# Attention matmuls on 128x32 column tiles in a four-layer convolution kernel

## The chip, the cores and the metric

The kernel runs on one core of a Trainium2 chip. The metric is the device time of one execution in microseconds (us), given as the median of several runs. A profile is one more execution, recorded by the hardware profiler.

## The reference

The input x is four images of 32 channels by 32x32 pixels, in float32. Four residual layers follow each other, each as x = x + layer(norm(x)), where norm normalises every channel of every image by its mean and variance:

```
x = x + L0(norm(x))   # second-order Volterra convolution 3x3: 9 taps and 45 products of tap pairs
x = x + L1(norm(x))   # 3x3 convolution (written with FFTs)
x = x + L2(norm(x))   # gated cell fed by attention
x = x + L3(norm(x))   # mixing of channels between two Hartley transforms
```

The change lies in the attention of L2. The cell's hidden state is zero, so one attention remains of four:

```
q = conv(xin, Wq, 'SAME')    # (4, 4 heads, 8, 1024 queries)
k = conv(xin, Wk, 'VALID')   # (4, 4 heads, 8, 900 keys)
v = conv(xin, Wv, 'VALID')
w = softmax(q^T k)           # over the 900 keys
a = v w^T
```

The gates i, g and o are then a projection of a, a bias and a sigmoid or a tanh, and the layer ends in a 32x32 projection.

## The kernel before

Five engines run their own instruction streams and meet at semaphores: TensorE (PE) does matrix products into PSUM, ScalarE (ACT) and VectorE (DVE) read PSUM, GpSimd (POOL) and SyncE (SP) issue copies, and POOL does some elementwise work.

The attention is computed for eight halves `s` (four images, two halves of 512 queries each). Queries and keys are split into three bfloat16 parts each, so that a product has 72 contraction rows and keeps float32 accuracy. For each half there are four kinds of PE work:

- Blocks of maxima (`max_block`, matmul at L1134): 128 queries against 450 keys. They find each query's maximum before the exponential. For each of the 16 pairs of head and query tile of a half there are two blocks. Either both are read by DVE, each by a reduction (L874), or the first is a product with the difference of two key halves, which goes through a ReLU on ACT (L669) and is then added to the second and reduced in one DVE instruction (L869). In halves 0 and 1 all 16 go by way of ACT, later 6 of 16.
- The turn (`turn_maxima`, L1141): the 48 columns of split maxima are transposed, so that they can be added to the contraction as three more rows. DVE copies the result and POOL issues a copy that places it.
- Score tiles (`score_tile`): 29 a half. 28 of them are 128 keys against 512 queries of one head (L1158); the 29th holds the 4 last keys of all four heads as four matmuls on 32 columns each (L1163). ACT takes the exponential of each (L661).
- Values (`values`): eight groups a half. The first seven have four matmuls, one head each, on 32 columns each (L1176); the eighth is one matmul on 128 columns (L1181). They are in float32, and the profile shows two instructions for each float32 matmul.

A PE instruction on the whole array is written 128*128 (or 72*128, rows in use by columns); one that uses 32 of the columns is written 128*32, and four of these address the four column strips of the array. Each matmul has a weight load (LDWEIGHTS, shown as the engine PEld) ahead of it.

The order of all this work is written out by `attention_plan()` (L132). A step of a half is four scores, of which the third is followed by the values of the step before, and between them 4.34 blocks of maxima (`BLOCKS_PER_STEP`) of the half after or the one after that. Every engine walks the same plan. Scores rotate over three PSUM banks (`SCORE_RING`), blocks of maxima and the turn over three others (`MAX_RING`), values over two. A score waits until the exponential of the third score before it has ended; a block waits until the block three before it has been read. Ahead of the first score 46 blocks and the first turn run, and 41 of these blocks are followed by a filler matmul on zeros (`keep_clock`). The gates (L1240, on 32 columns) and the output projection (L1248, on 128 columns) of the first 512 queries lie inside the last half.

Of the kernel before, what the change touches and what calls it, by code (L numbers as in the profile page):

```python
# [38 lines left out]
BF16 = mybir.dt.bfloat16  # L39
# [5 lines left out]
P = 128  # L45
B, C, H, W = 4, 32, 32, 32
# [43 lines left out]
HEADS, HC = 4, 8  # L90
# [3 lines left out]
KHALF = KEYS // 2  # L94
# [6 lines left out]
PARTS = 3  # L101
PAIR_ROWS = PARTS * PARTS * HC
S_ROWS = PAIR_ROWS + PARTS
HALF_TILES = HALF // P
ROWS_OF_MAX = HEADS * HALF_TILES
EXP_UNITS = HEADS * DT + 1
PRING = 8
# [24 lines left out]
def attention_plan():  # L132

    stream, i = [], 0
    for s in range(2 * B):
        for a in range(ROWS_OF_MAX):


            pair = s < 2 or a % 8 in (0, 3, 6)  # L150
            for kind in (("diff", "first") if pair else ("first", "second")):
                stream.append(("max", i, s, a, kind))
                i += 1
        stream.append(("split", s))
        if s == 2 * B - 1:
            stream += [("pause",)] * MOVED
        stream.append(("turn", i, s))
        i += 1

    for at in [at for at, item in enumerate(stream) if item[0] == "turn"]:  # L160
        if stream[at][2] == 0:
            continue
        n = min(MOVED, len(stream) - 1 - at)
        moved = stream[at + 1:at + 1 + n] + [stream[at]]
        numbers = sorted(item[1] for item in moved)
        stream[at:at + 1 + n] = [(item[0], k, *item[2:]) for item, k in zip(moved, numbers)]
    plan = []

    def take(n):

        while n > 0 and stream:
            item = stream.pop(0)
            if item[0] != "pause":
                plan.append(item)
            if item[0] != "split":
                n -= 1

    take(2 * ROWS_OF_MAX + 1 + FIRST_AHEAD)
    due, prev, later, step = 0.0, None, [], 0
    for s in range(2 * B):  # L180
        for t in range(DT + 1):
            units = HEADS if t < DT else 1
            due += BLOCKS_PER_STEP * (1.0 if t < DT else 0.6)
            taken = 0
            for h in range(units):
                plan.append(("score", s * EXP_UNITS + t * HEADS + h))
                k = int(due * (h + 1) / units + 1e-6)
                take(k - taken)
                taken = max(taken, k)
                if prev and h == min(2, units - 1):  # L190
                    plan.append(("values", *prev))
            due -= taken
            if prev and prev[1] == DT:
                later += [(step, ("read", prev[0])), (step + 1, ("write", prev[0]))]
                if prev[0] == 2 * B - 2:

                    later += [(step + 1, ("gates", 0)), (step + 2, ("cell", 0)), (step + 3, ("hidden", 0)),
                              (step + 4, ("out", 0))]
            plan += [item for at, item in later if at <= step]
            later = [(at, item) for at, item in later if at > step]  # L200
            prev = (s, t)
            step += 1
    plan += [("values", *prev)] + [item for _, item in later]
    plan += [("read", prev[0]), ("write", prev[0])]
    plan += [("gates", 1), ("cell", 1), ("gates", 2), ("hidden", 1), ("cell", 2), ("out", 1), ("hidden", 2),
             ("out", 2)]
    assert not stream
    return plan
# [28 lines left out]
def build(nc, x, consts, wmodes, max_rows, out):  # L237
    ctx = ExitStack()
    with ctx:
# [17 lines left out]
        vrest = sb("vrest", [P, B, P])  # L257
# [7 lines left out]
        mparts = sb("mparts", [P, PARTS, ROWS_OF_MAX], BF16)  # L265
        mt_sb = sb("mt_sb", [PARTS * ROWS_OF_MAX, P], BF16)
        ident_b = sb("ident_b", [P, P], BF16)
# [15 lines left out]
        qst = arena_a[:, 0:q_words].bitcast(BF16).rearrange("p (e g n) -> p e g n", e=2, g=G)  # L283
        kst = arena_a[:, q_words:q_words + k_words].bitcast(BF16).rearrange("p (g n) -> p g n", g=G)
# [9 lines left out]
        at = B * H * WP  # L294
# [7 lines left out]
        at = 8192 + PARTS * HW // 2  # L302
# [5 lines left out]
        probs = arena_b[:, 0:PRING * HALF].rearrange("p (s n) -> p s n", n=HALF)  # L308
# [7 lines left out]
        ps = ctx.enter_context(nc.psum_tensor("ps", [P, 8, 512], F32))  # L316
# [59 lines left out]
        max_scored = sem("max_scored")  # L376
# [55 lines left out]
            return maps[:, m, :].rearrange("p (y x) -> p y x", x=WP)[:, y0:y1_, x0:x1_]  # L432

        plan = attention_plan()
        prologue = 2 * ROWS_OF_MAX + WIDE_AHEAD

        def block_bank(i):

            ring = SCORE_RING + MAX_RING if i < prologue else MAX_RING
            return ring[i % len(ring)]  # L440
# [542 lines left out]
        def _(pe):  # L983
            mm = nc.tensor.matmul
# [63 lines left out]
            for i in range(3):  # L1048
                for r in range(3):
                    at = r * WP + i * PLANE  # L1050
                    last = mm(ps[32 * r:32 * r + 32, 2 + i, 0:PLANE], c_("bsel"), xp[:, at:at + PLANE],
                              start=True, stop=True)
# [3 lines left out]
            for e in range(2):  # L1056
                pe.wait_ge(planes_ready, e + 2)
                for px in range(3):
                    last = mm(ps[:, e, :].rearrange("p (y x) -> p y x", x=W), l1s[:, px, :],  # L1059
                              window(planes[0:96, :], 0, px, 16 * e, 16, W), start=(px == 0), stop=(px == 2))  # L1060
# [7 lines left out]
            for n in range(2 * B):  # L1068
                e, b = divmod(n, B)
# [48 lines left out]
            for h in range(HEADS):  # L1118
                last = mm(ps[32 * h:32 * h + KREST, 1, 3 * P:4 * P], vs[:, DT * P:KEYS], c_("ident"),
                          start=True, stop=True)  # L1120
# [4 lines left out]
            def max_block(i, s, a, kind):  # L1125

                before = block_before(i, block_bank(i))
                if before is not None:
                    pe.wait_ge(*blocks_read[before])
                e, b = divmod(s, B)  # L1130
                h, qt = divmod(a, HALF_TILES)
                g = b * HEADS + h
                at = {"first": 0, "second": KHALF, "diff": KDIFF}[kind]
                mm(ps[:, block_bank(i), 0:KHALF], qst[0:PAIR_ROWS, e, g, qt * P:(qt + 1) * P],  # L1134
                   kst[0:PAIR_ROWS, g, at:at + KHALF],
                   start=True, stop=True).then_inc(max_scored, 1)

            def turn_maxima(i, s):
                pe.wait_ge(*blocks_read[block_before(i, block_bank(i))])
                pe.wait_ge(m_split, s + 1)  # L1140
                nc.tensor.transpose(ps[0:PARTS * ROWS_OF_MAX, block_bank(i), 0:P // 2].bitcast(BF16),  # L1141
                                    mparts[:].rearrange("p s n -> p (s n)"), ident_b[:]).then_inc(max_scored, 1)

            def score_tile(n):

                half, i = divmod(n, EXP_UNITS)
                e, b = divmod(half, B)
                if i == 0:
                    pe.wait_ge(m_in, 16 * (half + 1))
                bank = SCORE_RING[n % len(SCORE_RING)]  # L1150
                if n >= len(SCORE_RING):
                    pe.wait_ge(expd, n - len(SCORE_RING) + 1)
                else:
                    pe.wait_ge(*blocks_read[block_before(prologue, bank)])
                if i < HEADS * DT:
                    t, h = divmod(i, HEADS)
                    g = b * HEADS + h
                    last = mm(ps[:, bank, :], kst[0:S_ROWS, g, t * P:(t + 1) * P], qst[0:S_ROWS, e, g, :],  # L1158
                              start=True, stop=True)
                else:  # L1160
                    for h in range(HEADS):
                        g = b * HEADS + h
                        last = mm(ps[32 * h:32 * h + 32, bank, :], kst[0:S_ROWS, g, DT * P:KPAD],  # L1163
                                  qst[0:S_ROWS, e, g, :], start=True, stop=True)
                last.then_inc(scored, 1)

            def values(half, t):

                n0 = half * EXP_UNITS + t * HEADS
                bank = O_RING[half % len(O_RING)]  # L1170
                if t == 0 and half >= len(O_RING):
                    pe.wait_ge(o_read, half - len(O_RING) + 1)
                if t < DT:
                    pe.wait_ge(expd, n0 + HEADS)
                    for h in range(HEADS):
                        last = mm(ps[32 * h:32 * h + 32, bank, :], vt[:, t, half % B * HEADS + h, :],  # L1176
                                  probs[:, (n0 + h) % PRING, :], start=(t == 0), stop=False,
                                  skip_group_check=True)
                else:
                    pe.wait_ge(expd, n0 + 1)  # L1180
                    last = mm(ps[:, bank, :], vrest[:, half % B, :], probs[:, n0 % PRING, :], start=False,  # L1181
                              stop=True, skip_group_check=True)
                last.then_inc(pv_done, 1)

            proj = c_("proj").rearrange("p (s o) -> p s o", o=32)
# [237 lines left out]
```

## Time and profile before

| | |
|---|---|
| Median of 3 runs | 330.51 us (330.33 to 331.64) |
| The profiled execution's own time | 330.47 us |
| Its span, first to last instruction | 328.7 us |
| PE busy | 303.6 us, 92% of the span |
| DVE, ACT, POOL busy | 209.6, 183.9, 30.2 us |
| Chain that ended last, by engine | PE 74%, DVE 14%, ACT 6%, issue 4%, DMA 1% |
| Chain by line, largest | L1176 16%, L1158 14%, L1134 12%, L1018 9% |

The attention, from its first score to its last values, lies between 107 and 283 us. A matmul's busy time is the time from its start to its modelled end, and matmuls overlap; so the distance from one start to the next tells more of PE than busy time does. A note in square brackets gives the idle time of the engine before the instruction and what ended it.

### The profile page before, as it was taken

Reading aid. Unit: us, or ns where it says so; the run is one execution under the profiler, and the core shown is the slowest. Engines: PE = TensorE matmul, PEld = TensorE weight load, DVE = VectorE, ACT = ScalarE, POOL = GpSimd, SP = SyncE. Lnnn points to the kernel's source line nnn. Section 1 sums busy time; section 2 is a strip of 40 time slices with the busy share of each in tenths; the row PEclk is TensorE's granted clock in tenths of the full one; section 3 lists DMA queues with packets and bytes.
Section 4 is the critical chain, followed back from the end, with each engine's and each line's share of the span. In section 5 each row is a group of like instructions: output and inputs, shape, how many; then the busy total and the mean of one; then the engine's idle time right before and its main releaser. Section 6 shows DMA issues by size and latency. Waiting matters only on the chain.

```text
span 328.7 us, 7306 instructions
## 1 busy us (share of the span) xinstructions
PE 303.6 (92%) x2956; PEld 121.4 (37%) x2956; DVE 209.6 (64%) x483; ACT 183.9 (56%) x346; POOL 30.2 (9%) x34
## 2 busy tenths in 40 slices
PE   5999999799998999999999999999999899897774
PEld 2685533234464222323223233232232222333651
DVE  4981264477288466977778769778787122367774
ACT  1111110224185997987877879778878788322800
POOL 6400000000000000100001001001010010800000
PEclk9999999999999999999999999999999999999799
DMA  7100000006750765930000000000000000000001
GB/s 237 51 6 2 4 12 0 2 0 179 161 106 6 154 159 153 341 166 2 1 2 2 1 2 2 0 3 3 2 2 0 2 3 0 2 0 3 2 4 64
DMA packets 3808, 15.10 MB, mean 46 GB/s; under 512 B 807, under 2 KB 1623, under 8 KB 3359
## 3 DMA queue, kind: packets, MB, share of 16 engines
q1 hardware_dynamic: 3519, 14.54, 15.4%
q8 instruction: 23, 0.38, 0.5%
q0 software_dynamic: 256, 0.11, 0.2%
q14 instruction: 10, 0.08, 0.1%
HBM read 12.17 MB, written 2.37 MB: 44 GB/s over the span
## 4 chain that ended last, share of the span: by engine, by line
PE 74%; DVE 14%; ACT 6%; issue 4%; DMA 1%; ACTq 0%; DVEq 0%
PE ps L1176 16%; PE ps L1158 14%; PE ps L1134 12%; PE ps L1018 9%; DVE sums L869 4%; ACT arena_b L661 4%; PE ps L989 4%; PE ps L1083 3%; PE ps L1295 3%; PE ps L1071 2%; PE ps L1181 2%; PE ps L1240 2%; PE ps L1059 2%; ACT relus L669 1%; ACT arena_a L690 1%
## 5 line engine op out<-in xcount | busy, mean ns | idle before, releaser
L661 ACT ACTIVATE arena_b<-ps 128x512 f32<-128x512 f32 x232 | 125.9, 608 | 29.9 <-PE ps L1158 29.0
L1134 PE MATMUL ps<-arena_a 72*128 72x450 bf16 x256 | 85.0, 355 | 2.3 <-DVE mx L869 1.6
L1158 PE MATMUL ps<-arena_a 75*128 75x512 bf16 x224 | 83.2, 383 | 1.3 <-ACT arena_b L661 0.8
L874 DVE TENSOR_REDUCE mx<-ps 128x1 f32<-128x450 f32 x120 | 68.9, 618 | 7.2 <-PE ps L1134 7.2
L869 DVE CUSTOM_DVE_ANT_0 sums<-ps,relus 128x450 bf16<-128x450 f32 x68 | 42.1, 625 | 32.5 <-PE ps L1134 29.7
L1176 PE MATMUL ps<-arena_b,vt 128*32 128x512 f32 x448 | 59.7, 605 | 0.7 <-ACT arena_b L661 0.7
L1158 PEld LDWEIGHTS ps<-arena_a 75*128 75x128 bf16 x224 | 21.3, 97 | 68.9 <-ACT arena_b L661 46.6
L989 PE MATMUL ps<-zeros 128*128 128x512 bf16 (+1 forms) x157 | 40.0, 366 | 4.8 <-DMA xa<-x 3.6
L669 ACT ACTIVATE relus<-ps 128x450 f32<-128x450 f32 x68 | 37.9, 557 | 9.4 <-PE ps L1134 8.1
L1134 PEld LDWEIGHTS ps<-arena_a 72*128 72x128 bf16 x256 | 24.6, 97 | 36.8 <-DVE mx L874 8.1
L1018 PE MATMUL ps<-arena_a,cst 32*32 32x512 f32 x720 | 26.0, 609 | 0.0
L989 PEld LDWEIGHTS ps<-zeros 128*128 128x128 bf16 x157 | 15.1, 100 | 21.7 <-issue 8.4
L1018 PEld LDWEIGHTS ps<-arena_a,cst 32*32 32x32 f32 x720 | 18.0, 103 | 6.0 <-issue 1.7
L619 ACT ACTIVATE arena_b<-ps 128x512 f32<-128x512 f32 x6 | 3.2, 600 | 27.4 <-PE ps L1018 27.4
L1083 PE MATMUL ps<-arena_b,cst 128*32 128x450 f32 (+1 forms) x144 | 15.9, 564 | 0.0
L690 ACT ACTIVATE arena_a<-arena_a 32x512 f32<-32x512 f32 x8 | 8.8, 1099 | 12.2 <-DVE arena_a L946 12.0
L731 DVE SCALAR_TENSOR_TENSOR arena_a<-xp 128x528 f32<-128x528 f32 (+6 forms) x24 | 15.1, 704 | 0.0
L1176 PEld LDWEIGHTS ps<-arena_b,vt 128*32 128x32 f32 x448 | 8.8, 108 | 15.7 <-ACT arena_b L661 9.4
L594 POOL DMA_DIRECT2D arena_a<-mt_sb x8 | 5.2, 646 | 102.1 <-DVE mt_sb L883 102.1
L891 DVE STREAM_TRANSPOSE ot<-ps 128x512 f32<-128x512 f32 x8 | 5.7, 708 | 12.7 <-PE ps L1181 12.7
L601 POOL TENSOR_TENSOR on<-ot,rden 128x512 f32<-128x512 f32 x7 | 7.3, 1039 | 60.8 <-DVE rden L893 60.8
L1295 PE MATMUL ps<-arena_b,arena_a 128*64 128x64 f32 x256 | 9.2, 245 | 2.0 <-ACT arena_a L690 2.0
(130 smaller groups left out, 226.3 us busy)
## 6 DMA issues: line engine op xcount, KB each, us to landing
arena_b<-wmodes SPq DMA_DIRECT2D x1, 4096.0 KB, 16.0
arena_a<-k_scratch SPq DMA_DIRECT2D x9, 258.4 KB
arena_a<-q_scratch SPq DMA_DIRECT2D x12, 96.0 KB
arena_a<-q_scratch SPq DMA_DIRECT2D x3, 384.0 KB
k_scratch<-arena_b SPq DMA_DIRECT2D x3, 344.5 KB, 3.6
cst<-consts SPq DMA_DIRECT2D x1, 901.0 KB, 8.0
arena_a<-k_scratch SPq DMA_DIRECT2D x6, 129.2 KB
q_scratch<-arena_b SPq DMA_DIRECT2D x6, 128.0 KB, 4.5
```

The source lines that it names most:

```text
L661: nc.scalar.activation(probs[:, n % PRING, :], ps[:, SCORE_RING[n % len(SCORE_RING)], :], ACT.Exp).then_inc(expd, 1)
L669: nc.scalar.activation(relus[:, d % 3, :], ps[:, block_bank(i), 0:KHALF], ACT.Relu).then_inc(max_relu, 1)
L731: nc.vector.scalar_tensor_tensor(map_box(m, e), image_box(m, e), VOLTERRA_SCALE, image_box(m, e, *PRODUCTS[m]), ALU.mult, ALU.mult).then_i ...
L869: nc.vector.tensor_tensor_reduce(out=sums[:, d % 2, :], in0=bank, in1=relus[:, d % 3, :], scale=1.0, scalar=-3.0e38, op0=ALU.add, op1=ALU.max,
L874: nc.vector.tensor_reduce(mx[:, a, e:e + 1], bank, AX.X, ALU.max).then_inc(max_read, 1)
L989: mm(ps[:, bank, 0:cols], zeros[:, 0:P], zeros[:, 0:cols], start=True, stop=True)
L1018: last = mm(ps[32 * j:32 * j + 32, B * e + b, :].rearrange("p (y x) -> p y x", x=HALF_COLS), weights[rows], window(image[rows], py, px + e ...
L1083: last = mm(ps[32 * b:32 * b + 32, bank + e, 0:ny * cols].rearrange("p (y x) -> p y x", x=cols), weights[:, px, :], window(xst[:, b, :], f ...
L1134: mm(ps[:, block_bank(i), 0:KHALF], qst[0:PAIR_ROWS, e, g, qt * P:(qt + 1) * P], kst[0:PAIR_ROWS, g, at:at + KHALF], start=True, stop=True ...
L1158: last = mm(ps[:, bank, :], kst[0:S_ROWS, g, t * P:(t + 1) * P], qst[0:S_ROWS, e, g, :], start=True, stop=True)
L1176: last = mm(ps[32 * h:32 * h + 32, bank, :], vt[:, t, half % B * HEADS + h, :], probs[:, (n0 + h) % PRING, :], start=(t == 0), stop=False, ...
L1295: last = mm(banks(4 * l2, 4)[64 * jh:64 * jh + 64, 64 * k:64 * k + 64].rearrange("p (l o) -> p l o", l=2), xm[:, l2, jh, k, :], wv[:, ls, ...
```

## The change

From the first score on, every score, every block of maxima, every turn and the eighth value group are issued as four (the turn: two) matmuls on 32 columns each, next to each other on the column strips, where there was one on the whole array. The blocks ahead of the first score, the first turn and the fillers stay as they were. Operands, results, PSUM banks, semaphores and the plan are the same; only the last matmul of each group signals. The output projection L1248 and all that follows the attention are not touched.

```diff
--- before.py
+++ after.py
@@ -432,6 +432,7 @@
             return maps[:, m, :].rearrange("p (y x) -> p y x", x=WP)[:, y0:y1_, x0:x1_]
 
         plan = attention_plan()
+        early_blocks = next(item[1] for item in reversed(plan[:plan.index(("score", 0))]) if item[0] == "max") + 1
         prologue = 2 * ROWS_OF_MAX + WIDE_AHEAD
 
         def block_bank(i):
@@ -1131,15 +1132,23 @@
                 h, qt = divmod(a, HALF_TILES)
                 g = b * HEADS + h
                 at = {"first": 0, "second": KHALF, "diff": KDIFF}[kind]
-                mm(ps[:, block_bank(i), 0:KHALF], qst[0:PAIR_ROWS, e, g, qt * P:(qt + 1) * P],
-                   kst[0:PAIR_ROWS, g, at:at + KHALF],
-                   start=True, stop=True).then_inc(max_scored, 1)
+                width = P if i < early_blocks else 32
+                for j in range(0, P, width):
+                    last = mm(ps[j:j + width, block_bank(i), 0:KHALF],
+                              qst[0:PAIR_ROWS, e, g, qt * P + j:qt * P + j + width],
+                              kst[0:PAIR_ROWS, g, at:at + KHALF], start=True, stop=True)
+                last.then_inc(max_scored, 1)
 
             def turn_maxima(i, s):
                 pe.wait_ge(*blocks_read[block_before(i, block_bank(i))])
                 pe.wait_ge(m_split, s + 1)
-                nc.tensor.transpose(ps[0:PARTS * ROWS_OF_MAX, block_bank(i), 0:P // 2].bitcast(BF16),
-                                    mparts[:].rearrange("p s n -> p (s n)"), ident_b[:]).then_inc(max_scored, 1)
+                rows = mparts[:].rearrange("p s n -> p (s n)")
+                width = PARTS * ROWS_OF_MAX if i < early_blocks else 32
+                for r0 in range(0, PARTS * ROWS_OF_MAX, width):
+                    r1 = min(r0 + width, PARTS * ROWS_OF_MAX)
+                    last = nc.tensor.transpose(ps[r0:r1, block_bank(i), 0:P // 2].bitcast(BF16), rows[:, r0:r1],
+                                               ident_b[:])
+                last.then_inc(max_scored, 1)
 
             def score_tile(n):
 
@@ -1155,8 +1164,10 @@
                 if i < HEADS * DT:
                     t, h = divmod(i, HEADS)
                     g = b * HEADS + h
-                    last = mm(ps[:, bank, :], kst[0:S_ROWS, g, t * P:(t + 1) * P], qst[0:S_ROWS, e, g, :],
-                              start=True, stop=True)
+                    for j in range(4):
+                        k0 = t * P + 32 * j
+                        last = mm(ps[32 * j:32 * j + 32, bank, :], kst[0:S_ROWS, g, k0:k0 + 32],
+                                  qst[0:S_ROWS, e, g, :], start=True, stop=True)
                 else:
                     for h in range(HEADS):
                         g = b * HEADS + h
@@ -1178,8 +1189,9 @@
                                   skip_group_check=True)
                 else:
                     pe.wait_ge(expd, n0 + 1)
-                    last = mm(ps[:, bank, :], vrest[:, half % B, :], probs[:, n0 % PRING, :], start=False,
-                              stop=True, skip_group_check=True)
+                    for h in range(HEADS):
+                        last = mm(ps[32 * h:32 * h + 32, bank, :], vrest[:, half % B, 32 * h:32 * h + 32],
+                                  probs[:, n0 % PRING, :], start=False, stop=True, skip_group_check=True)
                 last.then_inc(pv_done, 1)
 
             proj = c_("proj").rearrange("p (s o) -> p s o", o=32)
```

## Rows read from the trace of the kernel before

**Rows 1.** Stretches: length, busy us (instructions) of PE, PEld, DVE, ACT, POOL; granted clock; DMA.
```profile
107.00:131.57 24.57, 23.92 (x130) 7.08 (x130) 14.27 (x41) 21.91 (x46) 0.60 (x1) 1.00 0.65 157
...
175.85:198.06 22.21, 21.91 (x125) 6.79 (x124) 17.17 (x42) 17.80 (x36) 1.67 (x2) 1.00 0.01 2
...
242.47:264.97 22.50, 21.37 (x121) 5.86 (x120) 12.04 (x32) 18.61 (x37) 2.71 (x3) 1.00 0.01 2
264.97:283.00 18.03, 17.16 (x106) 4.38 (x103) 3.46 (x5) 13.97 (x27) 2.36 (x1) 1.00 0.00 1
```

**Rows 2.** PE timeline around a value group: start us, us, instruction.
```profile
179.90 0.35 PE L1134 MATMUL ps<-arena_a 72*128 72x450 bf16 x1
180.09 0.38 PE L1158 MATMUL ps<-arena_a 75*128 75x512 bf16 x1
180.31 0.35 PE L1134 MATMUL ps<-arena_a 72*128 72x450 bf16 x1
180.59 1.06 PE L1176 MATMUL ps<-arena_b,vt 128*32 128x512 f32 x8
181.59 0.39 PE L1158 MATMUL ps<-arena_a 75*128 75x512 bf16 x1
```

**Rows 3.** PE timeline, last score of a half and its eighth value group.
```profile
194.07 0.40 PE L1163 MATMUL ps<-arena_a 75*32 75x512 bf16 x4
194.40 0.63 PE L1134 MATMUL ps<-arena_a 72*128 72x450 bf16 x2
...
197.20 1.02 PE L1181 MATMUL ps<-arena_b,vrest 128*128 128x512 f32 x2
198.06 0.38 PE L1158 MATMUL ps<-arena_a 75*128 75x512 bf16 x1
```

**Rows 4.** PE timeline around a turn.
```profile
189.15 0.38 PE L1158 MATMUL ps<-arena_a 75*128 75x512 bf16 x1
189.45 0.24 PE L1141 MATMUL ps<-ident_b,mparts 128*48 128x128 bf16 x1
189.62 1.06 PE L1176 MATMUL ps<-arena_b,vt 128*32 128x512 f32 x8
```

**Rows 5.** Timelines of PE and PEld: convolution on 32 columns, groups of four.
```profile
74.41 1.04 PE L1083 MATMUL ps<-arena_b,cst 128*32 128x512 f32 x8
...
74.41 0.13 PEld L1083 LDWEIGHTS ps<-arena_b,cst 128*32 128x32 f32 x4 [0.30 <-issue]
...
74.84 0.13 PEld L1083 LDWEIGHTS ps<-arena_b,cst 128*32 128x32 f32 x4 [0.30 <-issue]
```

**Rows 6.** Line L1163 alone: ns min/median/max of one load, first and last start.
```profile
L1163 PEld LDWEIGHTS ps<-arena_a x32: 92/93/94, 127.6 to 280.2; 75*32 75x32 bf16 x32
```

**Rows 7.** DVE timeline of half 3.
```profile
175.34 0.63 DVE L869 CUSTOM_DVE_ANT_0 sums<-ps,relus 128x450 bf16<-128x450 f32 x1 [1.51 <-PE ps L1134]
...
178.44 1.69 DVE L874 TENSOR_REDUCE mx<-ps 128x1 f32<-128x450 f32 x3
...
181.41 0.63 DVE L869 CUSTOM_DVE_ANT_0 sums<-ps,relus 128x450 bf16<-128x450 f32 x1 [0.15 <-issue]
...
188.66 0.63 DVE L869 CUSTOM_DVE_ANT_0 sums<-ps,relus 128x450 bf16<-128x450 f32 x1
...
193.98 2.23 DVE L874 TENSOR_REDUCE mx<-ps 128x1 f32<-128x450 f32 x4 [0.16 <-PE ps L1134]
```

**Rows 8.** Timelines of ACT and PE in the first and the last two halves.
```profile
118.84 1.08 ACT L661 ACTIVATE arena_b<-ps 128x512 f32<-128x512 f32 x2 [0.19 <-PE ps L1158]
...
257.67 0.39 PE L1158 MATMUL ps<-arena_a 75*128 75x512 bf16 x1 [0.26 <-ACT arena_b L661]
...
271.20 3.52 ACT L661 ACTIVATE arena_b<-ps 128x512 f32<-128x512 f32 x7
```

**Rows 9.** Stretches inside L1295, columns as in rows 1.
```profile
307.70:311.10 3.40, 3.40 (x71) 3.40 (x68) 2.07 (x3) 3.08 (x3) 0.00 (x0) 0.50 0.00 0
311.10:315.90 4.80, 4.80 (x160) 4.64 (x157) 2.47 (x3) 0.00 (x0) 0.00 (x0) 1.00 0.02 3
```

## Prediction, written before the result was known

> **What bounds the kernel now.** I read the chain of waits first, by its shares, which the table of the profile shows: three quarters of the chain is PE, and the largest lines on it are the values, the scores and the blocks. Next I read busy time by stretch, to see how much room the other engines have. In a middle half of 22.21 us ACT is busy 17.80 and DVE 17.17; in the first half ACT is busy 21.91 of 24.57 [rows 1]. So PE sets the pace in the middle, ACT nearly does at the start, and neither neighbour is far behind. Last I read PE's timeline start by start, since starts and not busy times tell what a matmul occupies.
>
> On the whole array PE is at its pace already: a 450-column block is followed by the next matmul 0.19 us later and a 512-column score 0.22 us later [rows 2]. What isn't at pace is each visit to the column strips. The values start 0.28 us behind a block instead of 0.19, so entering costs 0.09. From the value group's start to the next score it takes 1.00 us [rows 2], while the eighth group, the same float32 columns on the whole array, takes 0.86 [rows 3]; so staying and leaving cost 0.14. The eighth group has the same switch of data type around it and pays nothing, so it is the change of tile shape that costs. A visit for values costs 0.23 us. L1163, bfloat16 on both sides, is left after 0.33 instead of 0.22 [rows 3]; with an entry of 0.09 it costs 0.20. The turn, on 48 columns, starts 0.30 behind a score (0.08 too much) and takes 0.17 where 128 moving columns at the score's rate take 0.055 [rows 4]; it costs 0.20, and this holds the entry of the values behind it.
>
> **The change part by part.**
>
> *Switches removed.* With everything on 128x32 strips, a middle half loses 7 times 0.14, 6 entries of 0.09, L1163 with 0.20 and the turn with 0.20: 1.92 us. Eight halves give 15.4. The gates in the last half lie between scores and lose their visit too (0.2), while L1248 stays on 128 columns and becomes a visit of its own (0.23), and one switch is needed at the first score (0.09). Gross: 15.2 us.
>
> *Matmuls added.* 224 scores and 210 blocks (256 less 46) become four matmuls each, seven turns become two each, and eight value groups four each. No row shows bfloat16 groups of four back to back. The nearest below: L1163's four start as one piece and leave after 0.33, which is 0.22 plus the exit of 0.11 that the values pay as well [rows 2, 3]. So the four strips stream at the same time, and a group costs what the single matmul did. Float32 groups back to back show the same: each group's loads and matmuls start 0.43 us after the last one's [rows 5], as one eighth-group instruction does (0.86 for two) [rows 3]. I take zero extra for each group. The upper end is a weight load that can't hide, 0.092 us a group [rows 6]; below zero nothing is to be had, because the stream of 512 columns is the same. I stay at zero since rows 5 are the nearest: there the loads for the next group start with the present group's matmuls (both at 74.41) on the same 128 rows, and the pitch holds.
>
> The Trainium skill ("TensorE: Matmul & The Clock Gate", section "The mechanism") says otherwise: a weight load overlaps running matmuls only if its row group differs, and all strips here share their rows. The trace contradicts it in rows 5, for float32; by that rule the sum would come out slower than before, which is the third rival below.
>
> *What is given back.* The neighbours were given 0.23 us a visit to catch up, and now aren't. I follow one middle half by the slack of each bank: how long before the matmul its bank had been read.
> First, DVE works without idle time from 175.34 until shortly before 181.41 [rows 7]. One value visit falls inside, ahead of the block at 180.31 [rows 2]. That block takes the bank that the last of three reductions reads until 178.44 + 1.69 = 180.13, a slack of 0.18. I allow 0.06 from a bank's release to the matmul that waits for it, so 0.12 is free and meets 0.23 saved: 0.11 given back.
> Second, the turn at 189.45 [rows 4] needs the bank whose reading ends at 188.66 + 0.63 = 189.29 [rows 7], a slack of 0.16, of which 0.10 is free. Since DVE last waited for PE, one value visit and the turn's entry have been saved there, 0.31: 0.21 given back.
> Third, the second block of the pair at 194.40 is late already (0.63 for the pair, 0.36 + 0.19 would do) [rows 3], held by the first reduction from 193.98, which had 0.16 of idle time ahead of it [rows 7]. A value visit and L1163 (0.43) meet that 0.16: 0.27 given back.
> Elsewhere DVE and ACT idle for 0.15 to 1.5 us a step and run along. So a middle half keeps 1.92 - 0.59 = 1.33 us; five of them keep 6.7.
>
> In the first half ACT's first idle time after the first score is 0.19 us before 118.84 [rows 8]; until there nothing but this 0.19 can be kept. The turn's second part, the values behind it, one more visit, L1163 and one more visit come where ACT idles again: 0.12 + 0.14 + 0.23 + 0.20 + 0.23. With 0.19 that is 1.1 us.
>
> The last two halves (242.47 to 283) have few or no blocks left. Scores there wait for exponentials (257.67 has 0.26 of PE idle ahead [rows 8]), but the visits lie on that same round, score, exponential, score, values, so they are kept. I count six full visits of 0.23 (1.38), three visits of which 0.11 of give-back comes off as above (0.58), the turn and the values behind it 0.34, the gates 0.20, two exits of 0.14 before which the values wait for an exponential (0.28), less L1248's 0.23. Two visits are worth nothing, because ACT works through from 271.20 for 3.52 us and just before that [rows 8]. The sum is 2.55.
>
> Sum: 1.1 + 6.7 + 2.55 = 10.35. One cost is left. A group's last matmul starts about 0.01 us after its first (0.40 for the four of L1163 against 0.39 for one score [rows 2, 3]), and this delays the reader wherever the reader waits for PE; some ten times a half, 0.8 us in all. Its bounds are 0 and, if every group of 434 paid it, 4.3. Net 9.6 us.
>
> The profiled execution took 330.47 us (328.7 of span and 1.8 around it), 0.04 below the median of the runs, so no correction is due: 330.5 - 9.6 = 320.9 us.
>
> **The rivals.**
>
> *All of it is kept.* DVE's and ACT's order adjusts and the three places cost nothing: 330.5 - 15.2 = 315.3. For it: both are idle more than 4 us in a middle half [rows 1]. Against it: the idle time doesn't lie where the slack is used up.
>
> *The neighbours take half.* With 1.92 us gone, a middle half of 20.3 us would have ACT at 88% and DVE at 85% busy, and the rings are three banks deep. If new waits come at the steps that look free now, twice the give-back (six halves times another 0.6, and the first half keeping nothing but 0.2) adds 4.5: 325.4.
>
> *Slower: weight loads don't hide.* A load for a strip whose rows are all streaming waits for the matmul. Then 434 groups pay up to 0.092 us [rows 6], 40 us, and the time is 330.5 - 15.2 + 40 = 355. It decides from 15.2 / 434 = 0.035 us a group, where the gain is used up; a smaller share of the same mechanism gives anything between. For it: no bfloat16 groups back to back are on record. Against it: rows 5.
>
> *It doesn't do what it says.* The switch is paid for something else (the change of stationary rows, 72 or 75 to 128), and stays: 330.5, give or take 1. Against it: the eighth group, with 128 rows between scores of 75, pays nothing [rows 3].
>
> Beside these, L1295 runs 3.40 us at a granted clock of 0.50 (1.2 GHz), 71 matmuls at 0.048 us against 0.030 behind it [rows 9]; PE idled ahead of it. An attention that ends earlier can move this or lose it, worth up to 1.3 us either way, and I leave the tail as it is.
>
> **How the numbers follow.** The forecast has 0.55, with its own range 318.5 to 323.5; all kept 0.15; half taken 0.16; slower 0.09; nothing changes 0.05. The range leaves out the slower rival, the no-change rival and the outer edges of the clock's movement: 315 to 327.5. Within 0.5% (1.65 us) a measurement of this kernel can hardly tell a change from none. Faster by more than that has 0.86, within it 0.05, slower 0.09.
>
> **What would show it.** In the changed kernel a value group's start should be followed by the next score's first matmul after 0.86 to 0.88 us instead of 1.00, and the values should start 0.19 to 0.20 us behind a block. Groups of four scores should be 0.22 us apart, with loads that start while the group before streams; 0.25 or more there makes the forecast wrong at once. A middle half should take about 20.9 us. New PE waits on DVE should stand before the block ahead of the second value group, before the turn and before the two blocks behind the half's last score. If these three are there and the half still takes 21.5 us or more, waits that I counted as free took the gain.

## The result, and the profile after

The changed kernel takes 320.77 us (median of 4 runs, 320.23 to 320.89) against 330.42 for the kernel before: a ratio of 0.9699, 95% interval 0.9671 to 0.9727. The forecast was 320.9. Run again in a later set it took 320.92 us, ratio 0.9696 (0.9668 to 0.9724). Here and below, a run more than 1.5% above the fastest of its kernel counts in the median but not in the ratio.

The profiled execution has a span of 318.4 us, 10.2 less than before. Its chain of waits, by engine and by line:

```profile
PE 68%; DVE 19%; ACT 5%; issue 5%; DMA 1%; DVEq 0%; ACTq 0%
```

PE's share fell from 74% to 68% and DVE's rose from 14% to 19%: PE became faster and waits more for DVE. Busy time by stretch, with the columns of [rows 1], follows. The first stretch starts at 107.00 us, 1.4 us ahead of the first exponential, and ends 1.7 us into the second half, as there; the second stretch has the length of one middle half:

```profile
107.00:131.24 24.24, 23.44 (x337) 8.43 (x341) 14.65 (x43) 22.19 (x46) 0.60 (x1) 1.00 0.60 138
172.42:193.28 20.86, 20.37 (x314) 8.01 (x310) 17.03 (x42) 17.79 (x36) 1.67 (x2) 1.00 0.01 3
```

The middle half went from 22.21 to 20.86 us. DVE and ACT have the same work in it (17.03 and 17.79 busy), in less time. In the first half ACT is still nearly the bound, with 22.19 of 24.24. PE's timeline shows the single steps; columns are start, length, instruction:

```profile
171.37 0.37 PE L1137 MATMUL ps<-arena_a 72*32 72x450 bf16 x4
171.56 1.04 PE L1193 MATMUL ps<-arena_b,vrest 128*32 128x512 f32 x8
172.42 0.40 PE L1169 MATMUL ps<-arena_a 75*32 75x512 bf16 x4
172.64 0.56 PE L1137 MATMUL ps<-arena_a 72*32 72x450 bf16 x8
173.02 0.40 PE L1169 MATMUL ps<-arena_a 75*32 75x512 bf16 x4
...
176.45 0.39 PE L1169 MATMUL ps<-arena_a 75*32 75x512 bf16 x4
176.78 0.37 PE L1137 MATMUL ps<-arena_a 72*32 72x450 bf16 x4
176.98 1.03 PE L1187 MATMUL ps<-arena_b,vt 128*32 128x512 f32 x8
177.84 0.39 PE L1169 MATMUL ps<-arena_a 75*32 75x512 bf16 x4
178.06 0.36 PE L1137 MATMUL ps<-arena_a 72*32 72x450 bf16 x4
```

The values now start 0.20 behind a block (176.78 to 176.98; 0.28 in [rows 2]) and are left after 0.86 (176.98 to 177.84; 1.00 before). A score group is followed after 0.22 (172.42 to 172.64), two block groups take 0.38 (172.64 to 173.02), which is 0.19 each. So groups of four cost what one whole matmul did. The weight loads, on the timeline of PEld:

```profile
172.42 0.33 PEld L1137 LDWEIGHTS ps<-arena_a 72*32 72x32 bf16 x8 [0.32 <-issue]
172.83 0.11 PEld L1169 LDWEIGHTS ps<-arena_a 75*32 75x32 bf16 x4
```

The block's loads start at 172.42, when the score's matmuls start, and the next score's load starts at 172.83, when the second block's matmuls do (0.19 ahead of 173.02). They run under matmuls on the same rows and add nothing.

The table gives the time by stages, each from the first exponential of a half (ACT, L661 before and L662 after) to that of the next, read from both traces, in us. Halves are counted from 0:

| stage | before | after | change | forecast |
|---|---|---|---|---|
| up to the first exponential | 107.69 | 108.37 | +0.68 | 0 |
| half 0 | 22.20 | 21.19 | -1.01 | -1.1 |
| halves 1 to 5 | 110.91 | 103.79 | -7.12 | -6.7 |
| halves 6 and 7, to the reading of the last values | 42.34 | 40.36 | -1.98 | -2.55 |
| what follows | 45.52 | 44.71 | -0.81 | 0 |
| span | 328.66 | 318.42 | -10.24 | -9.6 with 0.8 of stagger |

The first and the last row of changes aren't of the change's making. What precedes the first score is the same program, and the first blocks already stood 0.68 later. The last row is the granted clock: L1307 (L1295 before) ran at 1.00 throughout in this execution, where [rows 9] have 3.4 us at 0.50. In the repeated run's profile the low stretch was there again, and what follows took 45.52 us as it did before the change. The attention alone went from 175.45 to 165.34 us, a gain of 10.11, and to 165.33 in the repeat.

### The profile page after: what moved, and what is told of

It reads as the page before. It is cut to its first block, busy times and chain, and to the rows that moved or that the text cites. A ratio compares the mean times of both kernels' runs of the same rounds, so it can differ in the third digit from the quotient of the medians.

```text
span 318.4 us, 10018 instructions
## 1 busy us (share of the span) xinstructions
PE 290.8 (91%) x4308; PEld 128.7 (40%) x4316; DVE 208.9 (66%) x483; ACT 183.7 (58%) x346; POOL 30.2 (9%) x34
## 4 chain that ended last, share of the span: by engine, by line
PE 68%; DVE 19%; ACT 5%; issue 5%; DMA 1%; DVEq 0%; ACTq 0%
PE ps L1187 12%; PE ps L1137 12%; PE ps L1169 11%; PE ps L1019 9%; DVE sums L870 5%; PE ps L990 4%; ACT arena_b L662 3%; PE ps L1084 3%; PE ps L1307 2%; PE ps L1072 2%; PE ps L1193 2%; DVE mx L875 2%; PE ps L1252 2%; PE ps L1060 2%; ACT arena_a L691 1%
## 5 line engine op out<-in xcount | busy, mean ns | idle before, releaser
L662 ACT ACTIVATE arena_b<-ps 128x512 f32<-128x512 f32 x232 | 126.5, 617 | 20.3 <-PE ps L1169 18.6
L1137 PE MATMUL ps<-arena_a 72*32 72x450 bf16 (+1 forms) x889 | 87.7, 356 | 2.8 <-DVE mx L870 1.4
L1169 PE MATMUL ps<-arena_a 75*32 75x512 bf16 x896 | 85.9, 381 | 1.4 <-ACT arena_b L662 0.5
L1187 PE MATMUL ps<-arena_b,vt 128*32 128x512 f32 x448 | 58.3, 594 | 1.0 <-ACT arena_b L662 1.0
L1137 PEld LDWEIGHTS ps<-arena_a 72*32 72x32 bf16 (+1 forms) x889 | 27.1, 96 | 54.5 <-DVE mx L875 20.4
L990 PE MATMUL ps<-zeros 128*128 128x512 bf16 (+1 forms) x149 | 39.2, 371 | 5.7 <-DMA xa<-x 3.5
L670 ACT ACTIVATE relus<-ps 128x450 f32<-128x450 f32 x68 | 38.8, 570 | 9.4 <-PE ps L1137 8.1
L1169 PEld LDWEIGHTS ps<-arena_a 75*32 75x32 bf16 x896 | 24.0, 95 | 41.0 <-ACT arena_b L662 19.0
L1187 PEld LDWEIGHTS ps<-arena_b,vt 128*32 128x32 f32 x448 | 12.9, 110 | 7.1 <-ACT arena_b L662 3.0
L631 ACT ACTIVATE arena_b<-ps,cst 96x512 f32<-96x512 f32 x4 | 2.7, 685 | 14.1 <-PE ps L1072 14.1
```

Source lines behind the costliest of these rows:

```text
L662: nc.scalar.activation(probs[:, n % PRING, :], ps[:, SCORE_RING[n % len(SCORE_RING)], :], ACT.Exp).then_inc(expd, 1)
L670: nc.scalar.activation(relus[:, d % 3, :], ps[:, block_bank(i), 0:KHALF], ACT.Relu).then_inc(max_relu, 1)
L990: mm(ps[:, bank, 0:cols], zeros[:, 0:P], zeros[:, 0:cols], start=True, stop=True)
L1137: last = mm(ps[j:j + width, block_bank(i), 0:KHALF], qst[0:PAIR_ROWS, e, g, qt * P + j:qt * P + j + width], kst[0:PAIR_ROWS, g, at:at + KH ...
L1169: last = mm(ps[32 * j:32 * j + 32, bank, :], kst[0:S_ROWS, g, k0:k0 + 32], qst[0:S_ROWS, e, g, :], start=True, stop=True)
```

## The experiments

**Scores alone on strips.** This multiplies the changes of shape while half of the change stays.

```diff
-                width = P if i < early_blocks else 32        # blocks
+                width = P
...
-                width = PARTS * ROWS_OF_MAX if i < early_blocks else 32   # turn
+                width = PARTS * ROWS_OF_MAX
```
The comments are added here. The eighth value group is on the whole array as before; those lines are left out.

> Only the scores go to the column strips; blocks, turn and eighth value group stay on the whole array. Theory (each change of tile shape on PE costs 0.09 us on entering the strips and 0.11 to 0.14 on leaving): from the first score to the last values the order then has 392 changes of shape instead of 126, 58 in a middle half instead of 16. 196 visits at 0.20 are 39 us above the 315.3 us of the kernel with no change of shape: 352 to 356 us, slower than before by some 24 us, a middle half of about 25 us. Rival (narrower matmuls are themselves cheaper, whatever stands beside them): about half of the gain of the full change, 325 us.

Measured: 389.4 us in the fastest of four runs, 390.2 in the profiled one, 424 and 429 in the other two; ratio 1.1794 (1.1767 to 1.1821). It is slower, as the theory says and the rival doesn't, but by 59 us and not 24. What follows is of the profiled run. PE's timeline and two stretches:

```profile
257.65 0.40 PE L1169 MATMUL ps<-arena_a 75*32 75x512 bf16 x4
257.99 0.36 PE L1137 MATMUL ps<-arena_a 72*128 72x450 bf16 x1
258.28 0.40 PE L1169 MATMUL ps<-arena_a 75*32 75x512 bf16 x4
```
```profile
134.80:216.50 81.70, 81.69 (x376) 15.89 (x376) 33.37 (x76) 36.67 (x64) 3.35 (x4) 0.50 0.13 52
216.50:330.00 113.50, 112.21 (x944) 32.41 (x940) 71.34 (x164) 84.76 (x156) 7.73 (x9) 1.00 0.01 2
```

From a score to the block behind it, leaving the strips, takes 0.34, and from the block to the next score, entering them, 0.29, where 0.22 and 0.19 would do: the price per visit is that of before. At full clock, halves 4 and 5 took 25.9 us each (first exponentials at 247.76, 273.69 and 299.61), close to the 25 expected; that is 5.6 more than 22.21 - 1.92 = 20.29 without any visit, or 0.19 for each of 29 visits. The rest is the clock: for 81.7 us it was granted at 0.50 (1.2 GHz), and only 376 matmuls ran. At the rate of the full-clock stretch these need an estimated 376 / 944 x 113.5 = 45.2 us. Without the 36.5 lost the run would have taken 353.7 us. Counted by scores instead (53 of them took 81.3 us, and the same ones 46.5 in halves 3 and 4), 35 us were lost and it would have taken 355. Both estimates lie inside 352 to 356. So the price of a visit is shown at full clock, the total fits it, and the clock was not foreseen.

**Strips of 64 columns.** Scores and blocks are cut into two strips of 64 columns instead of four of 32. Not shown in the cut: the turn is one matmul on 48 columns, and the eighth value group is on two strips of 64.

```diff
-                width = P if i < early_blocks else 32
+                width = P if i < early_blocks else 64
...
-                    for j in range(4):
-                        k0 = t * P + 32 * j
-                        last = mm(ps[32 * j:32 * j + 32, bank, :], kst[0:S_ROWS, g, k0:k0 + 32],
+                    for j in range(2):
+                        k0 = t * P + 64 * j
+                        last = mm(ps[64 * j:64 * j + 64, bank, :], kst[0:S_ROWS, g, k0:k0 + 64],
```

> Scores, blocks and the eighth value group on two strips of 64 columns, the turn as one matmul on 48 columns, values as before on four strips of 32. Theory: it is equality of shape that counts, not smallness; 64 and 32 differ, so the visits stay: 330 us (328 to 332), value group to next score 1.00 us. Rival (smaller tiles, or more of them at once, make the gain): between 321 and 326 us.

Measured: 331.81 us, ratio 1.0018 (0.9983 to 1.0054), no different from the kernel before. PE around a value group:

```profile
178.27 0.36 PE L1137 MATMUL ps<-arena_a 72*64 72x450 bf16 x2
178.56 1.06 PE L1187 MATMUL ps<-arena_b,vt 128*32 128x512 f32 x8
179.55 0.41 PE L1169 MATMUL ps<-arena_a 75*64 75x512 bf16 x2
179.79 0.36 PE L1137 MATMUL ps<-arena_a 72*64 72x450 bf16 x2
```

It is entered after 0.29 and left after 0.99, as from the whole array (0.28 and 1.00). The strips of 64 themselves cost nothing that could hide a gain: between 176 and 240 us the median distance from a block to the next score is 0.193 us and from a score to the next block 0.219, as in the kernel before. Smaller tiles as such gain nothing; the neighbours have to have the same shape. The turn shows the same from the other side:

```profile
189.93 0.38 PE L1169 MATMUL ps<-arena_a 75*64 75x512 bf16 x2
190.15 0.22 PE L1149 MATMUL ps<-ident_b,mparts 128*48 128x128 bf16 x1
```

Behind a score on strips of 64 it starts after 0.22 instead of the 0.30 of [rows 4], so on 48 columns it is entered like a 64-column tile.

**The eighth value group back on the whole array.** This adds one change of shape and back a half, and nothing else:

```diff
-                    for h in range(HEADS):
-                        last = mm(ps[32 * h:32 * h + 32, bank, :], vrest[:, half % B, 32 * h:32 * h + 32],
-                                  probs[:, n0 % PRING, :], start=False, stop=True, skip_group_check=True)
+                    last = mm(ps[:, bank, :], vrest[:, half % B, :], probs[:, n0 % PRING, :], start=False,
+                              stop=True, skip_group_check=True)
```

> The changed kernel with the eighth value group alone back on the whole array, once a half. Theory: eight visits of 0.20 us are added, all where PE waits for nobody: 1.6 us more than the changed kernel, 322.4 us (322.0 to 322.7). Rival (a change of shape costs nothing by itself; what counted was the narrow form of scores and blocks): no change, 320.8 us.

Measured: 322.69 us, ratio 0.9757 (0.9722 to 0.9791), beside 320.92 for the changed kernel on the same chip: 1.77 more. The two intervals overlap (0.9696, 0.9668 to 0.9724), so the medians alone don't settle it. The trace does:

```profile
192.01 0.36 PE L1137 MATMUL ps<-arena_a 72*32 72x450 bf16 x4
192.30 1.12 PE L1192 MATMUL ps<-arena_b,vrest 128*128 128x512 f32 x2
193.36 0.40 PE L1169 MATMUL ps<-arena_a 75*32 75x512 bf16 x4
```

The eighth group, which paid nothing between whole-array matmuls in [rows 3] (0.86), is now entered after 0.29 and left after 1.06: a visit of 0.10 + 0.20, dearer than the 0.20 in all that was expected. The change of rows from 75 or 72 to 128 is the same in both kernels, so it isn't what costs. From the first exponential to the reading of the last values this execution took 167.67 us against 165.33, 2.34 more for eight visits, 0.29 each.

**Lighter DVE, in both kernels.** The plain reductions read half the columns, so the maxima leave out half the keys they cover; the exponential's argument is scaled by 0.01, in a line not shown:

```diff
-nc.vector.tensor_reduce(mx[:, a, e:e + 1], bank, AX.X, ALU.max).then_inc(max_read, 1)
+nc.vector.tensor_reduce(mx[:, a, e:e + 1], bank[:, 0:KHALF // 2], AX.X, ALU.max).then_inc(max_read, 1)
```

> The kernel before, with DVE's plain reductions reading 225 of 450 columns (the maxima are those of half the keys, and the exponential takes a hundredth of its argument so that nothing overflows). Theory: DVE is hardly waited for in this kernel; only the small waits ahead of two blocks a half go: 329 to 330 us. Rival (DVE sets the pace already): 325 us or less.

> The changed kernel with the same lighter reductions. Theory: what the change gave back, about 0.6 us a middle half ahead of the block before the second value group, ahead of the turn and ahead of the second last block of a half, is waiting for DVE; lighter reductions return it: 317 us (316 to 318), 12 to 13 us under the lightened kernel before. Rival (the give-back is ACT's, or PE's own cost of four matmuls a group): 320 to 321 us, as without it.

Measured: 328.42 us for the lightened kernel before, ratio 0.9937 (0.9913 to 0.9961), a little more gain than expected; and 316.66 for the lightened changed kernel, ratio 0.9583 (0.9555 to 0.9610), as expected; the distance between them is 11.8, just short of the 12 to 13 expected. A middle half of each, before and changed:

```profile
196.96:219.02 22.06, 21.76 (x125) 6.82 (x123) 13.17 (x42) 17.79 (x36) 1.68 (x2) 1.00 0.01 2
```
```profile
171.82:192.02 20.20, 19.89 (x314) 8.72 (x310) 12.88 (x42) 17.78 (x36) 1.68 (x2) 1.00 0.02 3
```

With DVE out of the way the change is worth 22.06 - 20.20 = 1.86 us a half, against 1.92 forecast gross; with DVE at full work it is 22.21 - 20.86 = 1.35, against 1.33 net. The lighter reductions return 0.66 us a half to the changed kernel and 0.15 to the one before. So what a half gave back is waiting for DVE. ACT has the same work in all four.

**A better balance.** The waits left point to where DVE is crowded. A seventh pair goes by way of ACT, and one of the six changes its place (15 instead of 14). The last version also takes three pairs of half 1 off ACT and puts the output projection inside the last half (L1248 before) on strips. The two new lines belong to two kernels; the comments are added, and the projection's lines are left out.

```diff
-            pair = s < 2 or a % 8 in (0, 3, 6)
+            pair = s < 2 or a in (0, 3, 6, 8, 9, 11, 15)                       # seven pairs
+            pair = s == 0 or (s == 1 and a not in (7, 10, 12)) or a in (0, 3, 6, 8, 9, 11, 15)   # last version
```

> The changed kernel once more, as the measure for the others of this set: 320.8 us.

> The changed kernel with seven instead of six of a half's 16 pairs going by way of ACT, and at other places (0, 3, 6, 8, 9, 11, 15 instead of 0, 3, 6, 8, 11, 14). Theory (the waits left are DVE's at two crowded places and one ReLU queued behind an exponential right after a value group): DVE has 0.55 us less a half, ACT 0.43 more, and the crowded places are relieved: 318 us (317 to 319.5). Rival (ACT becomes the bound): 321 us or more.

> As the one with seven pairs, and in half 1 three pairs (7, 10, 12) no longer go by way of ACT, and the output projection inside the last half is on strips too. Theory: ACT is the bound ahead of 118 us in the changed kernel, so three ReLUs less are worth up to 1.2 us there; the last visit but one goes, 0.2 us: 316.8 us (316 to 318.5). Rival: the first half is bound by DVE as much as by ACT, and only the 0.2 comes: 317.8 us.

Measured: 320.92 us for the changed kernel, 317.94 with seven pairs (five runs from 317.5 to 318.2 and one of 326.4; ratio 0.9607, 0.9580 to 0.9633), 317.04 for the last version (0.9605, 0.9564 to 0.9645). Moving pairs is worth some 3 us and beats both kernels. The last two can't be told apart by their ratios, but their traces show what the last step does: half 0 takes 19.99 us instead of 21.19, the 1.2 that the theory allowed, and from the first exponential to the reading of the last values it is 161.25 against 162.73. The middle half of the last version:

```profile
171.15:191.43 20.28, 20.11 (x318) 8.10 (x312) 16.66 (x42) 18.10 (x37) 1.68 (x2) 1.00 0.01 3
```

It took 20.28 us, as with seven pairs alone, and with ACT at 18.10 and DVE at 16.66 the load is shared better than at 17.79 and 17.03.

## Why the prediction was right

*Switches.* Prices and the count of visits held: 1.86 us a half where DVE doesn't interfere, against 1.92. That the shape and not the data type costs was argued from one row; strips of 64 and the eighth group back on the whole array show it. With that the rival in which nothing changes, because the rows are paid for, is out.

*Matmuls added.* Zero extra for a group was right, and the rival with loads that can't hide is out: 0.22 and 0.19 us a group, with loads under running matmuls on the same rows in bfloat16 too. The rule of the Trainium skill on row groups ("TensorE: Matmul & The Clock Gate", section "The mechanism"), which the forecast weighed, doesn't hold for these groups. The count was off by one: 45 blocks run ahead of the first score and stayed whole, 211 were cut (889 records of L1137 are 45 + 4 x 211).

*What is given back.* All three places appeared where they were named. The timeline of the changed kernel, one line each for the turn with its values, the two blocks behind a half's last score, and the score and block ahead of the second value group (above, 176.45 to 176.78):

```profile
184.93 0.39 PE L1169 MATMUL ps<-arena_a 75*32 75x512 bf16 x4
185.38 0.23 PE L1149 MATMUL ps<-ident_b,mparts 128*32 128x128 bf16 x2
185.40 1.07 PE L1187 MATMUL ps<-arena_b,vt 128*32 128x512 f32 x8
...
189.61 0.89 PE L1137 MATMUL ps<-arena_a 72*32 72x450 bf16 x8
```

The turn stands 0.45 behind a score instead of 0.22: 0.23 late, 0.21 forecast. The pair of blocks lasts 0.89 where 0.56 is undisturbed (at 172.64) and 0.63 was before: 0.26 lost, 0.27 forecast. The block at 176.78 is 0.33 behind its score instead of 0.22: 0.11 lost, 0.11 forecast. The sum, 0.60 us a half, goes with the lighter reductions, to within 0.06 of the gross. A middle half kept 1.35 us. The rival that all is kept asked for 1.92, and the one that the neighbours take half for some 0.7; both are out.

*What was off.* The last two halves kept 1.98 instead of 2.55. The term that was mis-sized is "the turn and the values behind it 0.34". In half 6 the last turn waits for the split of maxima, five small DVE instructions in a chain. PE and DVE, before the change:

```profile
255.06 0.39 PE L1158 MATMUL ps<-arena_a 75*128 75x512 bf16 x1 [0.26 <-ACT arena_b L661]
255.45 0.22 PE L1141 MATMUL ps<-ident_b,mparts 128*48 128x128 bf16 x1
```
```profile
255.13 0.17 DVE L853 TENSOR_TENSOR mparts<-negm,mparts 128x16 bf16<-128x16 f32 x1
```

And after it:

```profile
246.83 0.40 PE L1169 MATMUL ps<-arena_a 75*32 75x512 bf16 x4 [0.27 <-ACT arena_b L662]
247.45 0.23 PE L1149 MATMUL ps<-ident_b,mparts 128*32 128x128 bf16 x2 [0.22 <-DVE mparts L854]
```
```profile
247.13 0.18 DVE L854 TENSOR_TENSOR mparts<-negm,mparts 128x16 bf16<-128x16 f32 x1
```

In both kernels the turn starts 0.15 us after the split's last instruction has ended (0.147 by either trace, and no turn of these traces starts sooner behind its split). So it waited for the split already before the change, 0.39 behind its score instead of the 0.30 of [rows 4]. Counted from the half's first exponential, the split then came 0.54 us earlier and the score 0.78. The turn now starts 0.62 behind the score, 0.40 more than the score occupies, and from that score to the next it takes 1.52 us instead of 1.54 (255.06 to 256.60, 246.83 to 248.35): of the 0.34 only 0.02 was kept. The turn's slack for the split was never looked up. The other 0.25 that is missing in these two halves isn't traced to one place.

The stagger, booked at 0.8 us, costs nothing that can be found. A group's fourth matmul does start 0.01 us after its first, but halves 3 to 5 kept 1.35 each, where 1.33 was forecast without it. Without the 0.8 the forecast for the attention is 10.35, and 10.11 was measured: halves 1 to 5 kept 0.4 more than forecast, all of it in halves 1 and 2 (1.57 and 1.51), the last two 0.57 less and half 0 0.1 less. Why halves 1 and 2 kept more stays open.

That 320.9 met 320.77 so closely is partly luck. These errors and a stagger that wasn't there nearly cancel, and in the profiled execution two more shifts, outside the attention, do so too: the attention started 0.68 us later, and what follows it had no low stretch of clock and took 0.81 less.

## What to carry to other kernels

Before pricing a matmul, look at the shape of its neighbours: where whole-array and strip matmuls alternate, each visit costs 0.2 to 0.3 us here, and giving both the same shape removes it even if that means four times as many instructions. Half a conversion can be far worse than none. Then follow the slack of each buffer through one period: the gain stops where a neighbour was already working without a pause, and those places show what to rebalance next.

## What the runs showed of the hardware that was not expected

With scores on strips and blocks on the whole array, the granted clock stayed at 0.50 for 81.7 us although PE showed no idle time in them (81.69 us busy, with modelled ends). It fell at 134.6 us, during a PE wait of 2.25 us for a copy:

```profile
134.81 0.62 PE L1169 MATMUL ps<-arena_a 75*32 75x512 bf16 x4 [2.25 <-DMA arena_a<-mt_sb]
```

In five other profiles (the kernel before, the repeat, strips of 64, the lightened changed kernel and seven pairs) the clock fell once inside the program, 0.5 to 1.3 us after a PE wait of 2.0 us for ACT late in it, and came back after 3.4 us, as in [rows 9]. The other profiles with this wait, the first one of the changed kernel among them, kept the full clock behind it until the last 2.4 us. In the last version the clock fell elsewhere, at 285.56 us, behind PE waits of 1.25 and 0.71 us for DVE. In the scores-only kernel the same alternation of shapes ran at full clock from 216.5 us to the end of the attention. Why it recovered at that point, and whether the alternation is what kept it low, was not tried. In the runs at 424 and 429 us the mean granted clock was 0.80 and 0.79 against 0.89 in the profiled one.
